# Splitting the experts' weights into bf16 halves during the second stage's attention, and taking them from DRAM

## What is computed

```python
x = _layernorm(x + _L0_attn_ref(x, ...))            # stage 1, recurrent
x = _layernorm(x + _L0_xattn_ref(x, ctx_768, ...))  # stage 2, ternary weights, two attention layers, feed-forward
x = _layernorm(x + _L0_ffn_ref(x, ...))             # stage 3, mixture of experts
x = _layernorm(x + _L1_attn_ref(x, ...))
x = _layernorm(x + _L1_xattn_ref(x, ctx_768, ...))
x = _layernorm(x + _L1_ffn_ref(x, ...))

# stage 2, the part with attention, for each of two layers
kv = bitnet_linear(image_embeds, Wa, ba)
k = jnp.concatenate([kv, kv], axis=-1)
attn = softmax(einsum('bse,bpe->bsp', fused, k) / 16)
fused = fused + 0.1 * jnp.einsum('bsp,bpe->bse', attn, k)

# stage 3: E, K, D, F = 8, 2, 256, 1024
scores = xf @ Wg
w, idx = jax.lax.top_k(scores, K)
w = jax.nn.softmax(w, axis=-1)
xhat = (xf - mu) * jax.lax.rsqrt(var + EPS)
normed = xhat[None, :, :] * gamma[:, None, :] + beta[:, None, :]
h = jax.nn.relu(jnp.einsum('end,edf->enf', normed, W1) + b1[:, None, :])
out = jnp.einsum('enf,efd->end', h, W2) + b2[:, None, :] + xf[None, :, :]
y = jnp.einsum('ne,end->nd', cw, out)               # cw: w at the two chosen experts
```

## Time and profile before

| | us |
|---|---|
| median of 3 runs | 2793.13 (2791.08 to 2795.86) |
| the profiled execution | 2800.49 |
| its span in the trace | 2799.2 |
| attention layers 0 and 1, with their tails | about 361 to 485 and 505 to 635 |
| start of stage 3, from the barrier to the first transposes of a list tile | about 714 to 826 |
| main part of stage 3 | 830 to 1118 |

### The profile page before, as it was taken

The page is one execution under the profiler, slowest core; times in us unless marked ns, Lnnn a source line. Parts: engine busy times, 40 slices in busy tenths (PEclk is TensorE's granted clock), DMA queues, the critical chain, the costliest instruction groups (busy, mean ns, idle before and its releaser), DMA issues. The chain is left out here.

```text
span 2799.2 us, 41640 instructions
## 1 busy us (share of the span) xinstructions
PE 2197.8 (79%) x15624; PEld 1429.6 (51%) x15694; DVE 1667.9 (60%) x3395; ACT 1183.6 (42%) x2153; POOL 568.9 (20%) x489
## 2 busy tenths in 40 slices
PE   5987599896318999187789999995888686788677
PEld 3554167673317888144335555552555443455534
DVE  5866854568753333466666666634777542777663
ACT  2233834344232333042225555563665443566442
POOL 2110000001363544401210000002222232222052
PEclk9997799997558999588889999996998998899999
DMA  4113000100350111323321110102000001000100
...
DMA packets 81506, 118.22 MB, mean 42 GB/s; under 512 B 23396, under 2 KB 66368, under 8 KB 80832
## 3 DMA queue, kind: packets, MB, share of 16 engines
...
...
## 5 line engine op out<-in xcount | busy, mean ns | idle before, releaser
L2640 DVE TENSOR_REDUCE xa_max<-psum 128x1 f32<-128x1024 f32 (+1 forms) x256 | 248.4, 988 | 132.5 <-PE psum L2550 131.9
L2721 ACT ACTIVATE xa_work<-psum 128x1024 f32<-128x1024 f32 (+1 forms) x208 | 212.9, 1024 | 188.7 <-PE psum L2573 187.1
L2588 PE MATMUL psum<-xa_work,xa_values 128*33 128x128 f32 (+1 forms) x3328 | 223.9, 277 | 0.0
L2588 PEld LDWEIGHTS psum<-xa_work,xa_values 128*33 128x33 f32 (+1 forms) x3328 | 168.1, 111 | 73.7 <-issue 70.2
L2911 PE MATMUL psum<-wqkv_l,x_hl_l 128*128 128x512 bf16 x538 | 137.0, 401 | 65.5 <-POOL x_hl_l L3171 33.2
L3277 PE MATMUL psum<-h_ch_f,w_f 128*128 128x512 bf16 (+1 forms) x556 | 136.5, 400 | 34.8 <-issue 13.1
L1775 DVE TENSOR_SCALAR moe_raw<-psum,tile_b 128x256 f32<-128x256 f32 x184 | 78.3, 475 | 138.0 <-PE psum L1617 136.9
L1871 POOL TENSOR_TENSOR x_ch<-moe_raw,x_ch 128x512 bf16<-128x512 f32 x92 | 105.5, 1157 | 150.3 <-ACT x_ch L1831 148.2
L1617 PE MATMUL psum<-moe_rows,moe_w 128*128 128x256 bf16 x1104 | 131.8, 278 | 3.1 <-POOL moe_rows L1867 3.0
L2573 PE MATMUL psum<-xa_query_rows,xa_key_rows 98*128 98x512 bf16 (+1 forms) x416 | 127.2, 388 | 8.4 <-ACT xa_work L2721 7.7
L2550 PE MATMUL psum<-xa_key_rows,xa_query_rows 96*128 96x512 bf16 (+1 forms) x512 | 124.9, 339 | 8.9 <-ACT xa_work L2721 3.7
...
## 6 DMA issues: line engine op xcount, KB each, us to landing
...
moe_raw<-in_moe_w SPq DMA_DIRECT2D x16, 512.0 KB, 5.2
x_ch<-in_moe_w SPq DMA_DIRECT2D x16, 512.0 KB, 4.9
...
moe_rows<-slots_in SPq DMA_DIRECT2D x23, 256.0 KB, 3.1
slots_out<-moe_rows SPq DMA_DIRECT2D x23, 256.0 KB, 2.2
...
```

The source lines that it names most:

```text
L2588: ins = pe.matmul(total.ap[a * LANE:a * LANE + VC, c:c + PIECE], t["v"][b][0:rows, kt, first + a, :], exps[0:rows, a, c:c + PIECE], start= ...
L2640: v.tensor_reduce(t["maxes"][n % 2][:, qt * HU + a, part:part + 1], u.wide[:, 0:c1 - c0], AX.X, ALU.max).then_inc(*u.free)
L2721: act.activation(t["exps"][k % EXPS][0:rows], u.wide[0:rows].rearrange("p (m q) -> p m q", q=T), ACT.Exp, scale=1.0 / float(np.sqrt(np.flo ...
```

## The change

- In `attention_plan` each item gets two steps `("expert", i)`, so 64 in both layers. The pieces are now of 512 columns, 64 of them (`expert_part`). The two raw buffers and two buffers with both halves lie in `qx`, since `ternary_dve` now uses the destination tile itself for its scratch.
- ScalarE casts a piece (high half) at these two places of the item. GpSimd subtracts (low half). SyncE stores both halves of it into the new DRAM tensors `experts_1` and `experts_2`, in the layout of the SBUF tiles, and then loads piece i+2. The barrier behind each layer also waits for the stores.
- In stage 3 the splitting is gone from ScalarE, GpSimd and VectorE. SyncE loads both halves straight into place, 16 DMAs of 1 MB, four experts ahead of the wait for the gate and four behind it. TensorE waits for all 16.
- The gate's matmuls move into stage 2's feed-forward, ahead of the last transposes for groups 0 and 1, behind them for 2 and 3, in bank 0.
- In `experts_dve` the statistics stay, but reciprocal and normalisations come behind the slot addresses. GpSimd waits for each normalised tile by itself. The exponential of the gate comes behind the root on ScalarE.

```diff
@@ attention_plan
         plan += [("turn", layer, n, 0), ("turn", layer, n, 1), ("copy", layer, n, 0), ("copy", layer, n, 1)]
+        plan += [("expert", 2 * (ITEMS * layer + n))]
         plan += [("score", layer, n + 1, 0)] if more else []
...
-        plan += [("product", layer, n)]
+        plan += [("product", layer, n), ("expert", 2 * (ITEMS * layer + n) + 1)]
@@ bitnet
+                    expert_parts_sp(m, s, t, use, layer)
+                    expert_parts_pool(m, s, t, layer)
...
-                    settle(m, [use["later", layer, ITEMS - 1].done, use["turn", layer, ITEMS - 1, 2].done])
+                    settle(m, [use["later", layer, ITEMS - 1].done, use["turn", layer, ITEMS - 1, 2].done, s.e0_stored.now(), s.e1_stored.now()])
@@ expert_parts_sp
+    for i in range(steps * layer, steps * (layer + 1)):
+        _, dst = expert_part(m, i)
+        parts = t["expert_parts"][i % 2]
...
+        sp.wait_ge(*s.e_low(i + 1))
+        sp.dma_start(dst, parts).then_inc(*expert_stored(s, i).up(16))
+        if i + 2 < EXPERT_STEPS:
+            load(i + 2)
@@ expert_parts_pool
+    for i in range(steps * layer, steps * (layer + 1)):
+        parts = t["expert_parts"][i % 2]
+        g.wait_ge(*s.e_high(i + 1))
+        g.tensor_tensor(parts[:, 1, :], t["expert_raw"][i % 2], parts[:, 0, :], ALU.subtract).then_inc(*s.e_low.up())
@@ bitnet_attention_act
+        elif kind == "expert":
+            i, = step[1:]
+            act.wait_ge(*expert_loaded(s, i)(16 * (i // 2 + 1)))
+            if i > 1:
+                act.wait_ge(*expert_stored(s, i)(16 * (i // 2)))
+            act.copy(t["expert_parts"][i % 2][:, 0, :], t["expert_raw"][i % 2]).then_inc(*s.e_high.up())
@@ bitnet_ffn_pe
+    gate_pe(m, s, t, use, 0)
+    gate_pe(m, s, t, use, 1)
     pe.wait_ge(*s.normed(TILES))
     for h in range(HALVES):
         turn_pe(m, use["channels", B - 1, h], m.x_tok, B - 1, h)
+    gate_pe(m, s, t, use, 2)
+    gate_pe(m, s, t, use, B - 1).then_inc(*t["gate"].fill)
@@ gate_pe
+    for h in range(HALVES):
+        pe.wait_ge(*use["channels", g, h].done)
...
+    for tile in group(g):
+        for h in range(HALVES):
+            ins = pe.matmul(u.ap[:, tile * NE:(tile + 1) * NE], m.x_ch[:, h, tile * P:(tile + 1) * P], t["wg"][:, h, :],
+                            start=(h == 0), stop=(h == 1))
@@ experts_sp
+    for wait in split:
+        sp.wait_ge(*wait)
+    for e in range(NE):
+        if e == NE // 2:
             sp.wait_ge(*use["gate",].full)
...
+        sp.dma_start(t["w1"][:, e], dram["experts_1"][e]).then_inc(*s.w_loaded.up(16))
+        sp.dma_start(t["w2"][:, e], dram["experts_2"][e]).then_inc(*s.w_loaded.up(16))
@@ experts_pe
-    pe.wait_ge(*s.low_pool(POOL_PIECES))
-    pe.wait_ge(*s.low_dve(PIECES - POOL_PIECES))
+    pe.wait_ge(*s.w_loaded(16 * 2 * NE))
+    pe.wait_ge(*s.g_loaded(16))
@@ experts_dve
-    for p in range(POOL_PIECES, PIECES):
-        src, high, low = piece(t, p)
-        v.wait_ge(*s.split_high(p + 1))
-        v.tensor_tensor(low, src, high, ALU.subtract).then_inc(*s.low_dve.up())
@@ experts_act
-    split(0)
-    split(1)
+    act.wait_ge(*s.variance(TILES))
+    act.activation(m.std[:], m.mv[:, :, 1], ACT.Sqrt, bias=m.eps[:, 1:2]).then_inc(*s.deviation.up())
     act.wait_ge(*s.top_shifted(1))
     act.activation(t["sc"][:], t["sc"][:], ACT.Exp).then_inc(*s.top_exp.up())
-    for p in range(2, 6):
-        split(p)
...
-    for p in range(6, PIECES):
-        split(p)
+    act.wait_ge(*s.picked(3))
@@ experts_pool
-    for p in range(POOL_PIECES):
-        src, high, low = piece(t, p)
-        g.wait_ge(*s.split_high(p + 1))
-        g.tensor_tensor(low, src, high, ALU.subtract).then_inc(*s.low_pool.up())
     g.wait_ge(*s.addressed(1))
-    g.wait_ge(*s.normed(TILES))
     g.wait_ge(*m.slots.filled(16 * 3))
     for tile in range(TILES):
+        g.wait_ge(*s.normed(tile + 1))
```

132 lines of the change are left out of this document (74 added, 58 removed).

## The result

| | before | changed |
|---|---|---|
| median of 4 runs | 2794.5 (2791.1 to 2797.7) | 2763.2 (2760.7 to 2764.6) |
| ratio, 95% interval | | 0.989 (0.987 to 0.990) |
| profiled execution, its span | 2800.5, 2799.2 | 2763.1, 2761.8 |
| first transposes of a list tile | 825.98 | 795.75 |

The changed kernel is 31.3 us faster; 30.7 had been forecast. The stage marks agree with that: up to the first transposes of a list tile the trace has gained 30.2 us. The two profiled executions differ by 37 us, though, 6 more than the medians. That rest lies behind these transposes, in code which didn't change: 3 us in stage 3's main part and 4 behind it. In a second profile of the changed kernel the main part has its old length (292.9 us from the first transposes to the last product, 291.4 before, 288.4 in the first profile), so this is left out as chance.

What follows compares the result with a forecast made beforehand. Bound: gate products, VectorE's chain to slot addresses, 32 scatters, one load at the mixture of experts' start. Gains of 40.7 there less 10.0 in attention give -30.7, from the median 2793.1 to 2762.4 us; range 2750 to 2784.

Steps and rivals of the forecast that it cites:

- gate: Gate products moved into stage 2's feed-forward, filling TensorE's 3.52 us idle at the high clock: full 13.4 us earlier.
- chain to the first scatter: VectorE from gate to slot addresses: 18.9 us instead of 41.0, 22.1 earlier, without subtractions and with most normalisations moved.
- scatters: GpSimd's 32 scatters: 45.5 us instead of 50.7, gain 5.2, half the excess staying; ends 40.5 and 50.7.
- attention: Weight split moved into attention: steady items free, layer 1's quantising 1.5 us, two layer tails 8.5; cost +10.0, ends 5 and 14.
- four slow pieces: VectorE's chain: `chosen`, first `seen`, four sums and 16 normalisations, said to be slow because of GpSimd's subtractions.
- Loads of the weights: Stage 3: 21 MB with scatters take 63 us at about 334 GB/s, hidden by 8 us, charged nothing.
- Layer 0's tail: Behind attention layer 0, the barrier waits for the last store: 4.2 us late, last store issued at 487.1, taking 2.2.
- The clock (1): Rival: low clock at the gate, +7.0, or scatters held up as before, up to +5.2; 2768 to 2775 us; chance 0.15.
- The subtractions (2): Rival: GpSimd's subtractions meet VectorE's `softmax_bn` steps in attention, each waiting up to 1.16 us; +17, 2780 us; chance 0.12.
- The round trip (3): Rival: a raw buffer's round trip exceeds the 7.24 us attention item; +24, 2786 us (0.06), or +89, 2851 us (0.05).
- Loads that end last (4): Rival: stage 3's weight loads end at 786 instead of 777; +2 to +8, 2764 to 2770 us; chance 0.06.
- three signs of being wrong: Items over 7.5 us, casts waiting for DMA in mid-layer, or TensorE released by a weight load instead of a slot load.

Runs made afterwards that it cites:

- the old order: Changed kernel with the 16 normalisations back ahead of the placing of slot addresses; 2760.9 us, 0.991 of the kernel before.
- the short picks: Kernel without barrier waits for the attention layers' last stores, plus VectorE's 1472-column product cut into four of 368; 2754.8 us, again 2748.5, ratio 0.986 both times.
- the subtractions beside the ranking: Changed kernel plus twelve unused 128x1024 subtractions on GpSimd behind stage 3's barrier; 2780.2 us, 0.995 of the kernel before.
- no split: Kernel without barrier waits for last stores, plus the 64 weight pieces left out and experts' halves filled with constants; 2757.1 us, 0.986 of the kernel before.
- No wait: Changed kernel whose barriers behind the attention layers skip the last stores; ScalarE waits before the first hidden tile; 2745.1 us, again 2747.3, ratio 0.985 both times.

## Why the prediction was right, point by point

| step | forecast | trace |
|---|---|---|
| gate | -13.4 | -11.5 |
| chain to the first scatter | -22.1 | -22.3 |
| scatters | -5.2 | -7.3 |
| first list tile | 0 | 0 |
| attention | +10.0 | +10.9 |
| sum | -30.7 | -30.2 |

The parts are right in mechanism and mostly in size, but that the sum is off by only 0.5 is luck: gate and attention brought 2.8 us less than forecast, scatters and chain 2.3 more. The row of the attention also holds 0.3 by which the trace was behind when the attention began.

**Gate.** The first half is as reckoned: 32 records in 3.64 us, 114 ns each against 115, and transposes at the high clock. The term that was mis-sized is the other half: the clock fell in it, to 195 ns a record on average, and that is 1.9 us. My reason for the high clock, that the pause is filled, doesn't hold: the clock falls without a pause, and in eight of the twelve profiles it falls ahead of these transposes already.

**Chain.** 18.75 us against 18.9. The one cause named for four slow pieces was the right one: with 12 subtractions added, `seen` and the sums are slow again, and `chosen` is in part (0.68 instead of 0.36); with the old order, where the 16 normalisations take 5.26 us beside a quiet GpSimd instead of 16.19, 16.8 of the 22.3 us stay. I had taken 1.38/4 for a normalisation and 0.22 for the small operations, both from rows in which GpSimd did nothing, and both held.

**Scatters.** 43.5 us against 45.5. I had let half the excess stand because half of VectorE's work stays, as if the work's amount decided. The floor was 0.3 too high, for the last scatter has no gap behind it: 40.2. Of the 3.3 us over that, the scatter beside the product of 1472 columns alone makes 2.2 (2.1 by the short picks). The other five make 1.1, and 0.27 of it is due to the normalisations.

Here the Trainium skill (SBUF — State Buffer, "Who interferes with whom") infers that a tensor_tensor doesn't hold up the writing of descriptors. The rows before and after and the short picks speak against it: 0.96 alone, 3.15 beside one of 2.80, with its end 0.84 behind the product's. By its other rule, that an operation with two SBUF inputs waits for the whole of GpSimd's instruction and the reverse, the subtractions beside the ranking come out as measured (2.77 for 1.23, and up to 2.96 for GpSimd's 1.89).

**Loads of the weights.** Hidden, as forecast, and by some 25 us where 8 had been reckoned. They took from 724.5 to about 770 us, 46 us instead of 63; all transfers together reached 427 GB/s (760 to 765 us), where I had worked out 334.

**Attention.** 10.9 us against 10.0. Steady items were to cost nothing: 7.24 before and after, and "no split" puts all 64 pieces at 2.2 us. Layer 0's tail is 3.9 (TensorE waits 4.44 instead of 0.52), against 4.2. Its sum was wrong in two parts that nearly cancel. The last cast comes at 484.33, not 484.7, and its store is issued at 486.2, not 487.1; in return 2.9 us pass from there to TensorE's product, where I had 2.2. SyncE's timeline:

```profile
486.21 0.52 SPq L984 DMA_DIRECT2D experts<-text_q  x1
```

Layer 1's tail is 3.9 (TensorE waits 9.36 instead of 5.49 for `max_cols`), against 4.3. The meeting with layer 1's quantising costs 0.8, against 1.5. GpSimd is held up there, as reckoned, but what lengthens the item is VectorE's step, which is held up too (3.15 instead of 2.35). One term was missing. Behind the first tail the clock is low for a while: 0.9 us in the products, 0.8 up to layer 1's first exponential and 0.4 in its first item, 2.1 in all. "No wait" has none of it.

**Rivals.** The clock (1) came true for half of the gate and cost 1.9 of the 7 us; in other profiles with the early gate it costs up to 2.3 more. The scatters weren't held up as before. The subtractions (2) don't meet the steps on `softmax_bn` in layer 0, since they end 2 us ahead of these. Where they are made to, by doubling them, the step pays 0.53, as the rival said in kind, and half of it reaches the item. The round trip (3) was reckoned at 5.9 us. From a cast to the landing of the next load of its buffer it is 6.5 in the median of layer 0, and 8.05 at most. I had taken 7.24 as the point from which each microsecond more lengthens the item. Single trips above it don't: ScalarE's idle time takes them up. What lasting longer trips would cost no run shows. Loads that end last (4) didn't occur.

One of the three signs of being wrong that I had named did occur: five casts of layer 0 waited for their loads, for 0.20 to 0.40 us. It was too strict, since no item grew.

What stays open: why the clock falls where it does. The medians differ by 11 us for the early gate alone and for the removed waits, where the traces say 7 to 9; the intervals of these medians are wide enough for both. One profile is no better a measure of the whole, for the attention begins at 356.2 to 361.4 us in the fourteen profiles, behind stage 1, whose code all kernels share.

## What to carry to other kernels

Work on GpSimd that a trace shows as hidden can still be the cause of a slow chain on VectorE: compare the same form of instruction with GpSimd quiet and busy (0.22 against 2.16 here), and add up what the chain would take at the quiet price. When such work is moved beside another loop, the loop's items may be free while the barrier behind it is not: 8.7 of the 10.9 us paid came from waiting for the last store, 2 of them through TensorE's clock behind the pause, and one later wait, at the first use of the memory, took them away. An instruction of VectorE that can't be removed from beside descriptor writing can be cut in pieces at little cost (3.00 instead of 2.80 us here), though the 2 us that this gave the scatters didn't show in the medians. And a wait that a trace shows isn't yet a cost. With each subtraction doubled the casts waited up to 1.2 us for their loads and no item grew by that, while half a microsecond more in a step on one element a partition lengthened each.

## What the runs showed of the chip beyond expectation

- TensorE's granted clock fell from 1.00 to 0.50 while the engine was busy without a pause, with transposes and 128x8 fp32 products (720 to 729 us); the records of those products, two for each, stand 114 ns apart at the high clock, 215 at the low one.
- A scatter of 128 rows of 1 KB takes 0.96 us by itself, up to 3.15 beside one VectorE product of 2.80, and at most 1.17 beside the same product in four. The one that is held up ends 0.84 to 0.85 us behind the end of the product, wherever in it it began (three profiles).
- Beside subtractions on GpSimd without gaps, two-input operations of VectorE lengthen from 1.23 to 2.77 us and from 0.3 to 1.94 and more, while a reduction over 1024 columns keeps its 1.22. Even one on a single element a partition goes from 0.16 to 0.69 beside a subtraction.
- A 256 KB load lands in 3.8 us and a store in 3.0 where the two take turns during the attention, against 3.1 and 2.2 in stage 3.
